# Layer attention scores as three products of high and low parts, in place of fp32 products

## The chip, the cores and the metric

The kernel runs on one core of a Trainium2 chip. The metric is the device time of one execution in microseconds. Three executions of the kernel before gave 2423.75, 2425.5 and 2428.22 us, so the median is 2425.5 us.

## The reference

The program computes a modulated attention block over states of 4 x 1024 tokens and 256 channels, and then a block with two identical layers. Only those layers are touched here. In each layer a token's channels are shifted, projected to 8 heads of 64 channels, normalised and rotated, and every window of 128 tokens attends to itself and to the window before it:

```python
q = l2norm(q) * qs
k = l2norm(k) * ksc
q, k = rotary_xpos(q, k)
...
bq = q.reshape(b, h, w, WINDOW, d) * QK_SCALE
bk, bv = (look_around(bk), look_around(bv))     # the window and the one before it: 256 keys
sim = jnp.einsum('bhwid,bhwjd->bhwij', bq, bk)
...
sim = jnp.where(mask, -jnp.finfo(sim.dtype).max, sim)
attn = jax.nn.softmax(sim, axis=-1)
out = jnp.einsum('bhwij,bhwjd->bhwid', attn, bv)
```

The einsum that makes `sim` is the subject: for each window and head it multiplies 128 queries by 256 keys over 64 channels. After the attention of a layer come an output projection, a normalisation and a gated feed-forward part.

## The kernel before, in words

The function `phase_layers` handles both layers. A layer has 32 tiles of 128 tokens, one window each, and a loop over them in which every engine has its own program. Nothing is scheduled by a tool: the order of each engine's work is the order in which its block calls the small functions, and semaphores tie the engines together (`after(engine, name, n)` waits, `hold` waits and then counts a tick). The loop is pipelined over several tiles. While tile t is attended, the queries and keys of tile t+1 are rotated and transposed, tile t+2 is projected, and the stream of tile t+3 is transposed.

The parts that matter, with TensorE called PE, VectorE DVE, ScalarE ACT and GpSimd POOL:

- `qk_T` (PE, L1754) transposes the rotated queries of the next tile into the PSUM bank `ps_misc` and, a little later, its keys into the bank `ps_qkv[2]`.
- `copy_queries` (ACT, L1346) moves the queries to `qT` in SBUF and signals `qT_done`. `copy_keys` (DVE, L1534) moves the keys to `kT` and signals `kT_done`. `kT` has two halves, so that the window before stays at hand.
- `stream_T` (PE, L1731) writes to `ps_misc` again, so it waits for `qT_done`.
- `scores` (PE, L1762) does the products of two heads for one pair number j from 0 to 3. The first head has rows 0 to 63 of the array and its own PSUM bank, the second has rows 64 to 127 and another bank. Scores 0 and 1 of tile t+1 stand near the end of tile t, behind a wait for `kT_done`; scores 2 and 3 follow early in the next tile. In the text, the first group is scores 0 and 1 and the second group is scores 2 and 3.
- `maxima` (DVE, L1546 and L1549) adds the mask and takes row maxima, `exps` (ACT, L1355) exponentiates, `probs_T` (PE, L1773) transposes, `copy_probs` (ACT, L1363) copies, `values` (PE, L1783) multiplies by the values, and `reciprocals_T` (L1793), `copy_reciprocals` (ACT, L1367) and `normalise_out` (DVE, L1565) divide by the sums.
- `project_out` (PE, L1800) is the output projection, and `add_attended` (DVE, L1569) adds it to the stream. `squared_norms` (DVE, L1503 and L1505) follows on squares from ACT (L1342). The order of DVE in a tile is: rotate queries, normalise keys, maxima 2, `add_attended`, rotate keys, maxima 3, in every second tile a mask copy (L1671), squared norms, `copy_keys`, reciprocal sums, `stream_lo`, squared norms, maxima 0 and 1 of the next tile, `normalise_out`.

An fp32 product is one instruction in the program and two matmul records in the trace. Elsewhere in the kernel products are already made of high and low parts: a value x is rounded to the type fp32r (the high part), the low part is x less that, and `three_products` (L74 to L76) adds high by high, high by low and low by high.

Of the kernel before, what the change touches and what calls it, by code (L numbers as in the profile page):

```python
# [18 lines left out]
ALU = mybir.AluOpType  # L19
# [4 lines left out]
P = 128  # L24
# [1009 lines left out]
def phase_layers(nc, io, scr, keep):  # L1034
# [5 lines left out]
    with ExitStack() as ctx:  # L1040
# [37 lines left out]
        def cut(start, *shape, of=opnd):  # L1078
# [3 lines left out]
            if len(shape) > 1:  # L1082
# [3 lines left out]
        qT, o = cut(o + o % 2, 2, LP, P, of=plain)  # L1086
        kT, o = cut(o, LP, 2 * P, of=plain)
# [37 lines left out]
                 "h_hi ex_done sq_done pt_done rT_done qT_done v_done "  # L1125
# [5 lines left out]
        ACT_SEMS = "h_hi ex_done sq_done pt_done rT_done qT_done v_done w_hi_done warmed ff_done f_hi gl_done"  # L1131
        DVE_SEMS = ("mx_done nb_done h_lo rc_done rB_done oT_done red_done fl_done ra_done kn_done kT_done xa_done msk "
# [40 lines left out]
        with nc.Block() as block:  # L1173
# [42 lines left out]
            def _(pool):  # L1216
# [55 lines left out]
                for l in range(L):  # L1272
# [5 lines left out]
                    pool.memset(kT[:, :, P:2 * P], 0.0).then_inc(s["kz_done"], 1)  # L1278
# [44 lines left out]
            def _(act):  # L1323
# [20 lines left out]
                def copy_queries(l, t, par):  # L1344
                    hold(act, s["tick"], (s["qkT_mm"], at(2 * nth_rotated(l, t) + 1)))
                    act.activation(qT[:, par], ps_misc[:].rearrange("p (j q) -> p j q", j=LP), ACT.Copy).then_inc(s["qT_done"], 1)  # L1346
# [50 lines left out]
                for l in range(L):  # L1397
# [8 lines left out]
                    copy_queries(l, 0, 0)  # L1406
                    squares(l, 1, 1)
# [9 lines left out]
                    with act.Fori(0, B) as b, act.Fori(0, TB // 2) as jj:  # L1417
                        for par in range(2):
                            t = b * TB + jj * 2 + par
                            g = nth(l, t)  # L1420
                            exps(l, t, g, 0, par)
                            exps(l, t, g, 1, par)
                            copy_probs(g, 0)
                            copy_probs(g, 1)
                            copy_values(l, t + 2, (jj * 2 + par + 2) % V_RING)
                            exps(l, t, g, 2, par)
                            squares(l, t + 2, 1)
                            copy_queries(l, t + 1, 1 - par)
                            exps(l, t, g, 3, par)
                            copy_probs(g, 2)  # L1430
                            stream_hi(l, t + 3, 1 - par)
                            squares(l, t + 2, 0)
                            copy_probs(g, 3)
                            copy_reciprocals(g)
# [23 lines left out]
            def _(dve):  # L1458
# [73 lines left out]
                def copy_keys(l, t, par):  # L1532
                    after(dve, "qkT_mm", 2 * nth_rotated(l, t) + 2)
                    dve.tensor_copy(kT[:, :, par * P:(par + 1) * P],  # L1534
                                    ps_qkv[2][:].rearrange("p (j q) -> p j q", j=LP)).then_inc(s["kT_done"], 1)
# [89 lines left out]
                for l in range(L):  # L1625
# [14 lines left out]
                    if l == 0:  # L1640
                        last_shifts()
                    squared_norms(l, 1, 1)
                    copy_keys(l, 0, 0)
# [12 lines left out]
                    with dve.Fori(0, B) as b, dve.Fori(0, TB // 2) as jj:  # L1656
                        for par in range(2):
# [16 lines left out]
                            copy_keys(l, t + 1, 1 - par)  # L1674
# [48 lines left out]
            def _(pe):  # L1723
# [33 lines left out]
                def scores(l, t, j, par):  # L1757
                    if j % 2 == 0:
                        after(pe, "mx_done", 2 * nth_scores(l, t, j))
                    for h in range(2):  # L1760
                        rws = slice(h * DH, (h + 1) * DH)
                        step = pe.matmul(ps_s[h][:, (j % 2) * 2 * P:(j % 2 + 1) * 2 * P], qT[rws, par, j, :], kT[rws, j, :], start=True, stop=True,  # L1762
                                         skip_group_check=True)
                    step.then_inc(s["sc_mm"], 1)
# [263 lines left out]
```

## Time and profile before

| quantity | value |
|---|---|
| median of three executions | 2425.5 us |
| the profiled execution, its own time | 2426.99 us |
| its span, first to last instruction | 2425.2 us |
| mean granted TensorE clock | 0.98 of full |
| PE busy | 2288.2 us (94%) |
| PE weight loads (PEld) busy | 1753.3 us (72%) |
| DVE busy | 1957.4 us (81%) |
| ACT busy | 1551.4 us (64%) |
| POOL busy | 604.0 us (25%) |
| attention loop of the first layer | about 1031 to 1473 us of the span |
| attention loop of the second layer | about 1717 to 2180 us of the span |

The span leaves 1.8 us around it. PE is the busiest engine, but matmul records overlap each other, so a full PE row means only that it seldom waits. The distances between the starts of its records say more than their lengths. The two attention loops together take about 900 us, some 37% of the span; the rest is the first block (to about 990 us), two feed-forward parts and the output.

### The profile page before, as it was taken

The page shows a single profiled execution, that of the slowest core. Times are in us where ns is not written, and L with a number is a line of the kernel's source. Part 1 is how long each engine was busy: PE and PEld are TensorE (multiplying, and loading weights), DVE is VectorE, ACT ScalarE, POOL GpSimd, SP SyncE. Part 2 cuts the span into 40 slices and gives each one's busy share as a digit, 9 for nine tenths or more (in the row PEclk, how much of TensorE's full clock was granted, in tenths as well). Part 3 has the DMA queues.
Part 4 walks back from the last instruction along what each step waited for, and adds up shares of the span by engine and source line. Part 5 has one row for each costly group of instructions (what it writes and reads, how often), then busy time and mean ns, then how long its engine had stood idle before and what let it go on. Part 6 is the DMA issues. An engine that isn't in the chain of part 4 may idle for free. (4 is left out here: it accounts for less than half of the span.)

```text
span 2425.2 us, 63570 instructions
## 1 busy us (share of the span) xinstructions
PE 2288.2 (94%) x21268; PEld 1753.3 (72%) x21268; DVE 1957.4 (81%) x4606; ACT 1551.4 (64%) x3018; POOL 604.0 (25%) x692
## 2 busy tenths in 40 slices
PE   6999999999999999699999997999899999998994
PEld 4767776676777776577777776888677777776884
DVE  6999799979998998688888886666788888885666
ACT  5777577757776775377777674443677777773442
POOL 1000000000000000255555552222545454551110
PEclk9999999999999999899999998999999999998997
DMA  4000100010011001200000000001000000000004
GB/s 130 29 19 13 59 14 19 13 59 21 13 48 49 14 13 45 94 1 2 7 5 4 7 1 28 27 0 40 8 0 9 0 9 0 9 0 10 0 0 139
DMA packets 66986, 58.06 MB, mean 24 GB/s; under 512 B 3812, under 2 KB 64348, under 8 KB 66656
## 3 DMA queue, kind: packets, MB, share of 16 engines
q1 hardware_dynamic: 66912, 57.07, 7.5%
q8 instruction: 47, 0.77, 0.1%
q14 instruction: 27, 0.22, 0.0%
HBM read 44.47 MB, written 8.40 MB: 22 GB/s over the span
## 5 line engine op out<-in xcount | busy, mean ns | idle before, releaser
L599 ACT ACTIVATE at_p<-at_ps_s,at_shift 128x1024 f32<-128x1024 f32 (+3 forms) x384 | 335.7, 899 | 91.2 <-PE at_ps_s L800 49.9
L340 DVE TENSOR_TENSOR at_p_lo<-at_p,at_p_hi 128x1024 f16<-128x1024 f32 (+3 forms) x384 | 357.2, 951 | 5.5
L1355 ACT ACTIVATE ly_probs<-ly_masked,ly_small,ly_rq 128x256 f32<-128x256 f32 x512 | 301.4, 594 | 2.6 <-DVE ly_small L1549 1.4
L828 PE MATMUL at_ps_o<-at_v,at_p_hi 128*128 128x65 f16 x2304 | 238.1, 193 | 3.4 <-DVE at_p_lo L340 2.5
L1249 POOL TENSOR_TENSOR ly_rope_a<-ly_rope_a,ly_rope_t 128x512 f32<-128x512 f32 x132 | 168.8, 1278 | 285.5 <-DVE ly_rope_t L1517 285.5
L828 PEld LDWEIGHTS at_ps_o<-at_v,at_p_hi 128*128 128x128 f16 x2304 | 210.6, 96 | 39.7 <-issue 27.2
L829 PE MATMUL at_ps_o<-at_v,at_p_hi 128*128 128x64 f16 x2304 | 237.2, 194 | 0.0
L830 PE MATMUL at_ps_o<-at_v,at_p_lo 128*128 128x65 f16 x2304 | 236.1, 192 | 0.0
L335 DVE CAST at_p_hi<-at_p 128x1024 f16<-128x1024 f32 (+3 forms) x384 | 206.5, 556 | 25.8 <-ACT at_p L599 14.3
L1363 ACT ACTIVATE ly_operands_plain<-ly_ps 128x512 f32<-128x512 f32 x256 | 152.5, 596 | 102.5 <-PE ly_ps L1773 99.2
L830 PEld LDWEIGHTS at_ps_o<-at_v,at_p_lo 128*128 128x128 f16 x2304 | 212.4, 99 | 0.0
L829 PEld LDWEIGHTS at_ps_o<-at_v,at_p_hi 128*128 128x128 f16 x2304 | 212.1, 97 | 0.0
L1546 DVE CUSTOM_DVE_ANT_0 ly_masked<-ly_ps,ly_mask 128x256 f32<-128x256 f32 x520 | 199.1, 421 | 10.2 <-ACT ly_probs L1355 4.3
L74 PE MATMUL ly_ps<-ly_a_hi,ly_operands 128*128 128x512 f32 x408 | 180.9, 443 | 14.5 <-issue 9.1
L605 ACT ACTIVATE at_stage<-at_ps_m,at_bias 128x512 f32<-128x512 f32 x192 | 131.5, 685 | 77.5 <-PE at_ps_m L76 70.4
L1773 PE MATMUL ly_ps<-ident,ly_probs 128*128 128x128 f32 x1024 | 160.6, 279 | 16.0 <-ACT ly_probs L1355 15.7
L74 PE MATMUL at_ps_m<-at_hT,at_w_hi 128*128 128x512 f32 (+1 forms) x384 | 169.2, 441 | 5.9 <-DVE at_hT L390 3.0
L75 PE MATMUL ly_ps<-ly_a_lo,ly_operands 128*128 128x512 f32 x408 | 164.3, 403 | 0.0
L1773 PEld LDWEIGHTS ly_ps<-ident,ly_probs 128*128 128x128 f32 x1024 | 117.6, 140 | 64.5 <-issue 49.4
L76 PE MATMUL ly_ps<-ly_a_hi,ly_operands 128*128 128x512 f32 x408 | 163.0, 400 | 0.0
L1783 PE MATMUL ly_ps<-ly_operands_plain,ly_values 128*64 128x128 f32 x2048 | 154.2, 282 | 0.0
L75 PE MATMUL at_ps_m<-at_hT,at_w_hi 128*128 128x512 f32 (+1 forms) x384 | 152.7, 398 | 0.0
(238 smaller groups left out, 6242.2 us busy)
## 6 DMA issues: line engine op xcount, KB each, us to landing
at_w_raw<-in_Wv SPq DMA_DIRECT2D x32, 128.0 KB, 2.1
at_w_raw<-in_Wq SPq DMA_DIRECT2D x32, 128.0 KB, 2.3
at_w_raw<-in_Wk SPq DMA_DIRECT2D x32, 128.0 KB, 2.3
at_xio<-in_states SPq DMA_DIRECT2D x4, 1024.0 KB, 6.4
out_x<-x SPq DMA_DIRECT2D x4, 1024.0 KB, 9.5
out<-stream SPq DMA_DIRECT2D x4, 1024.0 KB, 7.9
ly_shifted<-stream SPq DMA_DIRECT2D x8, 508.0 KB
x<-at_xio SPq DMA_DIRECT2D x3, 1024.0 KB, 4.4
```

The lines of the kernel that those rows point to most:

```text
L74: pe.matmul(out, w_hi, x_hi, start=first, stop=False, skip_group_check=True)
L75: pe.matmul(out, w_hi, x_lo, start=False, stop=False, skip_group_check=True)
L335: dve.tensor_copy(p_hi[u % P_RING][:, :, off:], probs[u % P_RING][:, :, off:]).then_inc(p_hi_done, 1)
L340: dve.tensor_tensor(p_lo[u % P_RING][:, :, off:], probs[u % P_RING][:, :, off:], p_hi[u % P_RING][:, :, off:], ALU.subtract).then_inc(p_lo ...
L599: act.activation(probs[u % P_RING][:, :, off:], ps_s[u % 2][:, :, off:], ACT.Exp, bias=shift[:], scale=SCORE_SCALE).then_inc(exp_done, 1)
L828: pe.matmul(out, ph, ones_hi, start=(kt == 0 and t == 0), stop=False, skip_group_check=True)
L829: pe.matmul(out[:, 0:DH], ph, lo, start=False, stop=False, skip_group_check=True)
L830: step = pe.matmul(out, pl, ones_hi, start=False, stop=(kt == qc * CT + t), skip_group_check=True)
L1249: pool.tensor_tensor(ra[:, i, :], ra[:, i, :], rt[:, i, :], ALU.add).then_inc(s["add_done"], 1)
L1355: step = act.activation(pr[:, j % 2, h, :], sm[:, j % 2, h, :], ACT.Exp, bias=small[:, j % 2, 1, h:h + 1], scale=rq[:, par, 2 * j + h:2 * ...
L1546: dve.tensor_tensor_reduce(sm[:, j % 2, h, :], ps_s[h][:, half], mask[:, par].rearrange("p a b -> p (a b)"), 1.0, -3.0e38, ALU.add, ALU.ma ...
L1773: step = pe.transpose(ps_pt[:, (2 * slot + h) * P:(2 * slot + h + 1) * P], pr[:, j % 2, h, slot * P:(slot + 1) * P], ident[:])
```

## The change

The score products stop being fp32. Queries and keys are each kept as a high and a low part of type fp32r, and the score is the sum of high by high, high by low and low by high, accumulated in PSUM. The high parts are made by ACT (for the queries the same copy as before, now rounding; for the keys a new copy), the low parts by DVE, which subtracts the high part from the PSUM bank. `qT_done` and `kT_done` are now signalled by DVE. At the start of each layer the cleared half of `kT` is twice as large.

```diff
-        qT, o = cut(o + o % 2, 2, LP, P, of=plain)
-        kT, o = cut(o, LP, 2 * P, of=plain)
+        qT, o = cut(o + o % 2, 2, 2, LP, P)
+        kT, o = cut(o, 2, LP, 2 * P)
...
-                    pool.memset(kT[:, :, P:2 * P], 0.0).then_inc(s["kz_done"], 1)
+                    pool.memset(f32(kT[:, :, :, P:2 * P]), 0.0).then_inc(s["kz_done"], 1)
...
                 def copy_queries(l, t, par):
                     hold(act, s["tick"], (s["qkT_mm"], at(2 * nth_rotated(l, t) + 1)))
-                    act.activation(qT[:, par], ps_misc[:].rearrange("p (j q) -> p j q", j=LP), ACT.Copy).then_inc(s["qT_done"], 1)
+                    act.activation(qT[:, par, 0], ps_misc[:].rearrange("p (j q) -> p j q", j=LP), ACT.Copy).then_inc(s["qT_hi"], 1)
+
+                def copy_keys(l, t, par):
+                    after(act, "qkT_mm", 2 * nth_rotated(l, t) + 2)
+                    act.activation(kT[:, 0, :, par * P:(par + 1) * P],
+                                   ps_qkv[2][:].rearrange("p (j q) -> p j q", j=LP), ACT.Copy).then_inc(s["kT_hi"], 1)
...
                     copy_queries(l, 0, 0)
+                    copy_keys(l, 0, 0)
                     squares(l, 1, 1)
...
                             exps(l, t, g, 3, par)
                             copy_probs(g, 2)
+                            copy_keys(l, t + 1, 1 - par)
                             stream_hi(l, t + 3, 1 - par)
...
-                def copy_keys(l, t, par):
-                    after(dve, "qkT_mm", 2 * nth_rotated(l, t) + 2)
-                    dve.tensor_copy(kT[:, :, par * P:(par + 1) * P],
-                                    ps_qkv[2][:].rearrange("p (j q) -> p j q", j=LP)).then_inc(s["kT_done"], 1)
+                def low_queries(l, t, par):
+                    after(dve, "qT_hi", nth_rotated(l, t) + 1)
+                    dve.tensor_tensor(qT[:, par, 1], ps_misc[:].rearrange("p (j q) -> p j q", j=LP), f32(qT[:, par, 0]),
+                                      ALU.subtract).then_inc(s["qT_done"], 1)
+
+                def low_keys(l, t, par):
+                    after(dve, "kT_hi", nth_rotated(l, t) + 1)
+                    cols = slice(par * P, (par + 1) * P)
+                    dve.tensor_tensor(kT[:, 1, :, cols], ps_qkv[2][:].rearrange("p (j q) -> p j q", j=LP), f32(kT[:, 0, :, cols]),
+                                      ALU.subtract).then_inc(s["kT_done"], 1)
...
                     rotate_k(l, 0, 0)
                     if l == 0:
                         last_shifts()
+                    low_queries(l, 0, 0)
                     squared_norms(l, 1, 1)
-                    copy_keys(l, 0, 0)
+                    low_keys(l, 0, 0)
...
                             squared_norms(l, t + 2, 1)
-                            copy_keys(l, t + 1, 1 - par)
+                            low_queries(l, t + 1, 1 - par)
+                            low_keys(l, t + 1, 1 - par)
                             reciprocal_sums(g, par)
...
-                    for h in range(2):
-                        rws = slice(h * DH, (h + 1) * DH)
-                        step = pe.matmul(ps_s[h][:, (j % 2) * 2 * P:(j % 2 + 1) * 2 * P], qT[rws, par, j, :], kT[rws, j, :], start=True, stop=True,
-                                         skip_group_check=True)
+                    for n, (qx, kx) in enumerate(((0, 0), (0, 1), (1, 0))):
+                        for h in range(2):
+                            rws = slice(h * DH, (h + 1) * DH)
+                            step = pe.matmul(ps_s[h][:, (j % 2) * 2 * P:(j % 2 + 1) * 2 * P], qT[rws, par, qx, j, :], kT[rws, kx, j, :],
+                                             start=(n == 0), stop=(n == 2), skip_group_check=True)
                     step.then_inc(s["sc_mm"], 1)
```

How the instructions stand on the engines shows it at three places. The first is PE at the end of a tile: the transposes of the stream (`ly_xs`), values 1, the transposes of the probabilities 3, and then the first group of the next tile's scores. Before:

```order
L1731 MATMUL ly_ps<-ident,ly_xs 128x128 x2
L1783 MATMUL ly_ps<-ly_operands_plain,ly_values 64x128 x4
L1142 REGISTER_ALU
L1773 MATMUL ly_ps<-ident,ly_probs 128x128 x4
L1142 ISA
L1762 MATMUL ly_ps<-ly_operands_plain 128x256 x4
L1783 MATMUL ly_ps<-ly_operands_plain,ly_values 64x128 x8
```

The same place on PE now, where `ly_operands` is the area of type fp32r:

```order
L1746 MATMUL ly_ps<-ident,ly_xs 128x128 x2
L1799 MATMUL ly_ps<-ly_operands_plain,ly_values 64x128 x4
L1142 REGISTER_ALU
L1789 MATMUL ly_ps<-ident,ly_probs 128x128 x4
L1142 ISA
L1778 MATMUL ly_ps<-ly_operands 128x256 x12
L1799 MATMUL ly_ps<-ly_operands_plain,ly_values 64x128 x8
```

Nothing else moved on PE; the group has 12 instructions in place of 4, which were fp32. The second place is DVE between the squared norms and the reciprocal sums. Before:

```order
L1503 TENSOR_REDUCE ly_norm<-ly_sq 128x8
L1505 TENSOR_SCALAR ly_norm<-ly_norm 128x8
L1142 REGISTER_ALU
L1534 COPY ly_operands_plain<-ly_ps 128x4x128
L1142 REGISTER_ALU
L1555 RECIPROCAL ly_rsum<-ly_sums 128x8
L1557 COPY ly_operands_plain<-ly_rsum 128x512
```

On DVE now:

```order
L1510 TENSOR_REDUCE ly_norm<-ly_sq 128x8
L1512 TENSOR_SCALAR ly_norm<-ly_norm 128x8
L1541 TENSOR_TENSOR ly_operands<-ly_ps,ly_operands 128x512
L1547 TENSOR_TENSOR ly_operands<-ly_ps,ly_operands 128x4x128
L1142 REGISTER_ALU
L1568 RECIPROCAL ly_rsum<-ly_sums 128x8
L1570 COPY ly_operands_plain<-ly_rsum 128x512
```

One copy became two subtractions, first the queries' and then the keys'. The third place is ACT after the last exponentials of a tile, from the copy of probabilities 2 to the squares. Before:

```order
L1363 ACTIVATE ly_operands_plain<-ly_ps 128x512
L50 REGISTER_ALU
L50 ISA
L50 REGISTER_ALU
L1336 ACTIVATE ly_operands<-ly_ps 128x128
L1337 ACTIVATE ly_operands<-ly_ps 128x128
```

On ACT now:

```order
L1368 ACTIVATE ly_operands_plain<-ly_ps 128x512
L1142 REGISTER_ALU
L1350 ACTIVATE ly_operands<-ly_ps 128x4x128
L50 REGISTER_ALU
L50 ISA
L50 REGISTER_ALU
L1336 ACTIVATE ly_operands<-ly_ps 128x128
L1337 ACTIVATE ly_operands<-ly_ps 128x128
```

ACT has one more copy per tile (L1350, the high part of the keys), between the copy of probabilities 2 and `stream_hi`.

## Rows read from the trace of the kernel before

**Rows 1.** One line's instructions, the mask copy of every second tile: count, length, first and last start.

```profile
L1671 DVE COPY ly_mask<-ly_prev_mask x16: 216/216/216, 1047.9 to 1471.4; 128x128 f32 x16
...
L1671 DVE COPY ly_mask<-ly_prev_mask x16: 214/216/216, 1736.3 to 2176.3; 128x128 f32 x16
```

**Rows 2.** Timeline of PE over one tile: start, length, engine, operation, count.

```profile
1291.15 1.13 PE L1762 MATMUL ly_ps<-ly_operands_plain 64*128 64x256 f32 x8
...
1303.33 0.60 PE L1754 MATMUL ly_ps<-ident,ly_rope_a 128*128 128x128 f32 x4
1303.77 0.38 PE L1731 MATMUL ly_ps<-ident,ly_xs 128*128 128x128 f32 x2
...
1305.26 1.13 PE L1762 MATMUL ly_ps<-ly_operands_plain 64*128 64x256 f32 x8
1306.32 1.09 PE L1783 MATMUL ly_ps<-ly_operands_plain,ly_values 128*64 128x128 f32 x16
```

**Rows 3.** Timelines of PE and its weight loads (PEld): other kinds of product.

```profile
1296.77 1.89 PE L1800 MATMUL ly_ps<-ly_operands_plain 128*128 128x256 f32 x8
...
1503.95 0.28 PE L75 MATMUL ly_ps<-ly_f_lo,ly_operands 128*128 128x256 f32 x1
1504.07 0.28 PE L76 MATMUL ly_ps<-ly_f_hi,ly_operands 128*128 128x256 f32 x1
...
600.68 0.34 PE L800 MATMUL at_ps_s<-at_q1hi,at_k1hi 64*128 64x384 f16 x2
600.85 0.33 PE L800 MATMUL at_ps_s<-at_q1lo,at_k1hi 64*128 64x384 f16 x2
...
1305.79 0.19 PEld L1762 LDWEIGHTS ly_ps<-ly_operands_plain 64*128 64x128 f32 x2
```

**Rows 4.** Timeline of DVE over the same tile; in brackets idle time before and releaser.

```profile
1289.87 0.69 DVE L1534 COPY ly_operands_plain<-ly_ps 128x512 f32<-128x512 f32 x1 [1.04 <-PE ly_ps L1754]
...
1297.99 0.16 DVE L1549 SCALAR_TENSOR_TENSOR ly_small<-ly_small,ly_rq 128x2 f32<-128x2 f32 x1
1298.88 0.42 DVE L1569 TENSOR_TENSOR stream<-stream,ly_ps 128x256 f32 x1 [0.73 <-PE ly_ps L1800]
...
1302.42 0.69 DVE L1503 TENSOR_REDUCE ly_norm<-ly_sq 128x8 f32<-128x512 f32 x1 [0.23 <-DVE ly_mask L1671]
1303.15 0.17 DVE L1505 TENSOR_SCALAR ly_norm<-ly_norm 128x8 f32<-128x8 f32 x1
1303.97 0.69 DVE L1534 COPY ly_operands_plain<-ly_ps 128x512 f32<-128x512 f32 x1 [0.65 <-PE ly_ps L1754]
```

**Rows 5.** Timeline of ACT: two copies in a row, and probabilities 2.

```profile
1285.08 0.60 ACT L1363 ACTIVATE ly_operands_plain<-ly_ps 128x512 f32<-128x512 f32 x1 [1.57 <-PE ly_ps L1773]
1285.57 0.59 ACT L1350 ACTIVATE ly_values<-ly_ps 128x512 f32 x1
...
1303.60 0.60 ACT L1363 ACTIVATE ly_operands_plain<-ly_ps 128x512 f32<-128x512 f32 x1
```

**Rows 6.** Timelines of ACT, DVE and PE at two handovers between engines.

```profile
1308.14 0.60 ACT L1367 ACTIVATE ly_operands_plain<-ly_ps 128x512 f32<-128x512 f32 x1 [2.12 <-PE ly_ps L1793]
...
1308.78 0.69 DVE L1565 TENSOR_TENSOR ly_operands_plain<-ly_ps,ly_operands_plain 128x512 f32<-128x512 f32 x1 [0.23 <-ACT ly_operands_plain L1367]
...
1691.73 0.28 DVE L1496 TENSOR_TENSOR ly_operands<-ly_ps,ly_operands 128x128 fp32r<-128x128 f32 x1
...
1692.11 0.74 PE L74 MATMUL ly_ps<-ly_a_hi,ly_operands 128*128 128x512 f32 x1 [1.33 <-issue]
```

**Rows 7.** Second layer: ACT's timeline, and PE's waits from 1740 to 2180 us.

```profile
1772.33 1.28 ACT L1355 ACT_TABLE_LOAD   x1
...
PE ly_ps L1773 <- ACT ly_probs L1355: 15.7, 15, 1.2
```

**Rows 8.** Timelines of ACT and DVE ahead of the first layer's loop.

```profile
1016.73 0.60 ACT L1342 ACTIVATE ly_sq<-ly_ps 128x512 f32<-128x512 f32 x1 [1.86 <-PE ly_ps L76]
...
1018.16 0.68 DVE L1534 COPY ly_operands_plain<-ly_ps 128x512 f32<-128x512 f32 x1
```

More of the change, by code:

```diff
@@ L1124, in phase_layers @@
                  "xT_mm qkv_mm sc_mm pt_mm pv_mm qkT_mm rT_mm wo_mm "
-                 "h_hi ex_done sq_done pt_done rT_done qT_done v_done "
+                 "h_hi ex_done sq_done pt_done rT_done qT_hi kT_hi qT_done v_done "
                  "mx_done nb_done h_lo rc_done rB_done oT_done red_done fl_done ra_done kn_done kT_done xa_done msk "
@@ L1130, in phase_layers @@
         PE_SEMS = "xT_mm qkv_mm sc_mm pt_mm pv_mm qkT_mm rT_mm wo_mm fT_mm gu_mm y_mm"
-        ACT_SEMS = "h_hi ex_done sq_done pt_done rT_done qT_done v_done w_hi_done warmed ff_done f_hi gl_done"
-        DVE_SEMS = ("mx_done nb_done h_lo rc_done rB_done oT_done red_done fl_done ra_done kn_done kT_done xa_done msk "
+        ACT_SEMS = "h_hi ex_done sq_done pt_done rT_done qT_hi kT_hi v_done w_hi_done warmed ff_done f_hi gl_done"
+        DVE_SEMS = ("mx_done nb_done h_lo rc_done rB_done oT_done red_done fl_done ra_done kn_done qT_done kT_done xa_done msk "
                     "w_lo_done rope_q bn ag vr nr xnd f_lo uf_done u_lo ya_done")
```

## The prediction

> **What bounds the kernel now.** I read the mask copy's starts first, because it runs once in two tiles and so gives the period of the loop [rows 1]. In the first layer 15 pairs of tiles take 1471.4 - 1047.9 = 423.5 us, or 14.12 us a tile. In the second layer they take 440.0 us, or 29.33 us a pair: 1.1 us more for each pair. Then I read PE through a tile. From one first group of scores to the next, 1291.15 to 1305.26, is 14.11 us [rows 2], and in the first layer's loop PE's timeline shows no idle time that another engine causes. DVE, by contrast, waits for PE: 0.73 us ahead of `add_attended`, 0.65 or 1.04 us ahead of the copy of keys [rows 4]. So PE is the bound of the first layer. In the second layer ACT loads an activation table of 1.28 us once in a pair, and PE waits 15.7 us in 15 waits for the exponentials behind it, 1.05 us a pair [rows 7]. There ACT is the bound for a short stretch, between the first and the second group of scores' followers. The change makes PE's score groups shorter, lengthens the way from transposed keys to scores, and gives DVE one more operation. I count these in turn, on a clock that starts at 0 with a first group of scores.
>
> **Score groups on PE.** A group before takes 1.06 us to the start of what follows (1305.26 to 1306.32), in 8 records of 1.13 us together [rows 2]. The output projection has records of the same width over all 128 rows: 8 of them take 1.89 us [rows 3]. The seven steps between starts are thus (1.89 - 1.13) / 7 = 0.109 us shorter in the scores. That fits when the two heads run beside each other: an unpaired step of 0.217 us, and a pair of records in 0.217 us. A group is then 4 pair steps, 0.87 us, and 0.19 us of start and handover that I leave as they are.
>
> Now a group has 12 instructions, 6 pairs of one pass each. No row shows fp32r products on 64 rows. The nearest is the first block's f16 scores, also two heads on 64 rows: a pair with 384 columns is followed by the next after 0.17 us [rows 3], which for 256 columns makes 0.113 us. fp32r with 256 columns on all rows steps by 0.12 us [rows 3]. Paired, 6 steps are 0.68 us (with 0.12 us: 0.72; with half of 0.217: 0.65), so a group saves 0.19 us, with ends of 0.15 and 0.22. Unpaired, 12 steps of 0.12 are 1.44 us, and a group costs 0.57 us more. I take 0.19, as the row with two heads and one pass is the nearest in kind. Two groups a tile save 0.38 us.
>
> **The way of the keys.** Before, DVE took up the transposed keys at 1303.97 and the scores began at 1305.26, 1.29 us later, without waiting: the transposes of the stream, values 1 and probabilities 3 filled that time. Now ACT copies first. It starts its copy of probabilities 2 at 1303.60, and its next copy can start 0.49 us later [rows 5], at 1304.09, 0.12 us after the keys are there. The copy takes 0.60 us, the handover to DVE 0.04 us (1308.14 + 0.60 to 1308.78), a DVE operation on a PSUM bank and SBUF 0.69 us, and the handover from DVE to PE 0.10 us (1691.73 + 0.28 to 1692.11) [rows 6]. The sum is 0.12 + 0.60 + 0.04 + 0.69 + 0.10 = 1.55 us. The slack that hid the old copy is used up, and the scores wait 0.26 us. Behind them in PE's queue stand values 2 and 3 and all of the next tile. The ends are 0.12 us (if ACT is free at once and handovers cost nothing) and 0.40 us. Without a mask copy, a first-layer tile thus changes by -0.38 + 0.26 = -0.12 us.
>
> **The way of the queries, and DVE.** `stream_T` now waits for a subtraction on DVE. DVE starts on the keys 0.79 us ahead of the scores, at -0.79. From there to where it is free for `add_attended` was 1298.15 - 1289.87 = 8.28 us [rows 4], the subtraction being as long as the old copy: 7.49. PE had the projection ready at 1298.88 - 1291.15 = 7.73, and now has it at 7.35, so DVE's wait of 0.73 us is gone and DVE itself is 0.14 us late. From `add_attended` to the end of the squared norms (1298.88 to 1303.32) are 4.44 us in a tile with the mask copy: 11.93. With 0.69 and 0.10 the low queries reach PE at 12.72, where PE wants to start the transposes of the stream at 1303.77 - 1291.15 - 0.38 = 12.24. PE waits 0.48 us there, and 1.49 us later, at 14.21, the scores begin. The keys alone would have allowed 12.82 - 0.38 + 1.55 = 13.99. So the tile with the mask copy takes 14.21 us, 0.10 us more than before. In the other tile the mask copy and the wait behind it (0.44 us together) are missing, and the queries come in time. The pair changes by -0.02 us, the 16 pairs of the first layer by -0.3 us.
>
> **The second layer.** In the tile with the table load PE waits for ACT after its second group of scores, and the table load hangs on ACT's last copy of the tile before, which only the first group brings forward. The second group's saving falls into PE's wait of 1.05 us. The tile changes by -0.19 + 0.26 = +0.07 us, the one with the mask copy again by +0.10, and 16 pairs by +2.7 us.
>
> **Ahead of each loop.** ACT's copy of the keys now stands ahead of squares that DVE waits for, and DVE's keys wait for it too. Before, the squares began as soon as PE had finished a projection, at 1016.73, and the keys' copy at 1018.16 ran right before the first scores [rows 8]. One ACT copy of 0.60 us and a handover in the chain make 0.75 us a layer by my estimate, 1.5 us in all, between 0 and twice 1.39 us (a copy, a subtraction and a handover in line). The larger clearing on POOL is covered: the keys come much later. The extra ACT copy inside the loop is covered by ACT's waits for PE, of which [rows 5] shows one of 1.57 us; the copy of probabilities 3 has to wait for PE's transposes anyway.
>
> **Sum.** -0.3 + 2.7 + 1.5 = +3.9 us. The profiled execution took 2427.0 us by its own time (span 2425.2), which makes 2430.9; against the median of 2425.5 it makes 2429.4 us.
>
> **Rivals.**
>
> 1. The handovers stay hidden and the whole saving lands. For it: DVE and ACT both have idle time. Against it: the slack that counts is 1.29 us, and three operations in line don't fit. First layer 32 x 0.38 = 12.2 us, second 16 x (0.19 + 0.38) = 9.1 us, less 1.5: 2405.7 us.
> 2. The heads don't pair in fp32r: slower. Price 0.57 us a group. For it: no row has this kind on 64 rows. Against it: both fp32 and f16 pair [rows 2, 3]. First layer 32 x (1.14 + 0.26) = 44.8 us; second, where one group's loss hides in the wait for ACT, 16 x (0.83 + 1.40) = 35.7 us; with 1.5: 2507.5 us. It decides as soon as a pair takes more than about 0.15 us.
> 3. The weight loads limit the pairs. A pair of loads is recorded with 0.19 us [rows 3]; until now a pair of products of 0.217 us covered it, and 0.113 us would not. If pairs step by 0.19, a group is 1.14 us, 0.27 more: 32 x 0.80 + 16 x 1.33 + 1.5 = 48.4, or 2474 us. Against it: part of a record is lead-in, since the fp32 pairs show no gap. The Trainium skill, "TensorE: Matmul & The Clock Gate", Part 3, says that a weight load overlaps a matmul in flight only when its row group differs. Here each head's next load has its own head's product in flight; by that rule a pair would cost load and product in line, 0.19 + 0.217 = 0.41 us before, and four pairs 1.63 us, where the whole group took 1.06. The trace does not agree for fp32.
> 4. DVE becomes the bound of every tile. It has lost its wait ahead of `add_attended`, and in the tile with the mask copy it sets the pace already. If its stretches of 8.28 and 4.44 us grow by 0.1 us each, for instance as operations meet POOL's, it costs 0.2 us in each of 64 tiles, 12.8 us more than the forecast: 2442 us.
>
> **Chances and range.** The forecast, with errors of a few us around it, 56 in 100; DVE as the bound 19; unpaired heads 10; the full saving 6; loads as the limit 4; something that I don't see 5. 0.1 us a tile are 6.4 us, and 0.2% of the time, what a measurement of this kernel can tell from no change, are 4.9 us. The forecast lies inside that and close to its upper edge. The range is 2418 to 2446 us: below lies the full saving, above unpaired heads and loads. From the same cases: faster 0.09, no change 0.41, slower 0.50.
>
> **What would show it.** In the profile after, a first group of scores should be some 0.87 us long to the next start, with pairs about 0.11 to 0.12 us apart. DVE's wait ahead of `add_attended` should be gone in the first layer, PE should show new waits ahead of the stream's transposes in every second tile and ahead of the scores in the others, and the mask copies should stand 28.2 us apart in the first layer and 29.5 us in the second. The forecast is wrong if groups take over 1.06 us, if PE has no new wait, or if the queries' subtraction is late in both kinds of tile.

## The result and the profile after

The changed kernel takes 2433.3 us (median of 9 executions, 2429.0 to 2433.5), the kernel before 2424.0 us (median of 9, 2422.3 to 2428.2) on the same chip. The ratio is 1.0032, with a 95% interval of 1.0022 to 1.0043: 7.8 us slower by the ratio, with 5.3 to 10.4 (the two medians lie 9.3 us apart). The forecast was 3.9 us slower, below that interval, and its range of 2418 to 2446 us holds the measured time. Every ratio in this text is to the kernel before on the same chip. The profiled execution took 2431.27 us by its own time (span 2429.2, mean granted clock 0.98 as before).

The first rows are the busy times on the page of the changed kernel, and then the mask copy of every second tile, which answers to [rows 1].

```profile
PE 2273.0 (94%) x21788; PEld 1762.2 (73%) x21788; DVE 1988.6 (82%) x4672; ACT 1573.8 (65%) x3084; POOL 602.1 (25%) x692
```

```profile
L1685 DVE COPY ly_mask<-ly_prev_mask x16: 214/215/271, 1045.2 to 1470.5; 128x128 f32 x16
L1685 DVE COPY ly_mask<-ly_prev_mask x16: 214/215/216, 1736.6 to 2179.4; 128x128 f32 x16
```

PE has 15 us less of busy time and the kernel is slower, so PE waits somewhere it did not. The mask copies divide the difference by place. The first number is taken from DVE's first weight subtraction of the layers, which starts at 996.0 us before and at 993.0 after:

| stretch | before, us | after, us | difference |
|---|---|---|---|
| weight subtraction to first mask copy | 51.9 | 52.2 | +0.3 |
| 15 pairs of tiles, first layer | 423.5 | 425.3 | +1.8 |
| from loop to loop | 264.9 | 266.1 | +1.2 |
| 15 pairs of tiles, second layer | 440.0 | 442.8 | +2.8 |
| last mask copy to the end | 248.9 | 249.8 | +0.9 |
| sum | 1429.2 | 1436.2 | +7.0 |

The first block, which the change doesn't touch, ran 3 us shorter in this one profile, and so the two own times are only 4.3 us apart. In a second profile of the same changed kernel the subtraction starts at 995.6 us. The sum of the table is the number to hold against the medians.

PE over a pair of tiles, which answers to [rows 2]: start, length, engine, line, operation, count, idle time before with its releaser.

```profile
1289.95 0.98 PE L1778 MATMUL ly_ps<-ly_operands 64*128 64x256 f32 x12 [0.20 <-DVE ly_operands L1547]
1290.85 1.09 PE L1799 MATMUL ly_ps<-ly_operands_plain,ly_values 128*64 128x128 f32 x16
...
1301.82 0.60 PE L1769 MATMUL ly_ps<-ident,ly_rope_a 128*128 128x128 f32 x4
1302.70 0.41 PE L1746 MATMUL ly_ps<-ident,ly_xs 128*128 128x128 f32 x2 [0.28 <-DVE ly_operands L1541]
...
1304.21 0.98 PE L1778 MATMUL ly_ps<-ly_operands 64*128 64x256 f32 x12
1305.12 1.09 PE L1799 MATMUL ly_ps<-ly_operands_plain,ly_values 128*64 128x128 f32 x16
...
1318.31 0.39 PE L1778 MATMUL ly_ps<-ly_operands 64*128 64x256 f32 x2 [0.20 <-DVE ly_operands L1547]
```

A score group now lasts 0.90 to 0.91 us to the start of the next work (1289.95 to 1290.85, 1304.21 to 1305.12) where it lasted 1.06. The two new waits stand in the brackets: for the queries' low part (L1541) in the tile with the mask copy, for the keys' low part (L1547) in the other. The tile with the mask copy takes 1304.21 - 1289.95 = 14.26 us, the other 1318.31 - 1304.21 = 14.10 us.

DVE and ACT in the same pair, which answer to [rows 4] and [rows 5].

```profile
1289.11 0.69 DVE L1547 TENSOR_TENSOR ly_operands<-ly_ps,ly_operands 128x512 fp32r<-128x512 f32 x1 [1.19 <-ACT ly_operands L1350]
1297.37 0.42 DVE L1582 TENSOR_TENSOR stream<-stream,ly_ps 128x256 f32 x1 [0.28 <-PE ly_ps L1816]
1300.97 0.69 DVE L1510 TENSOR_REDUCE ly_norm<-ly_sq 128x8 f32<-128x512 f32 x1 [0.23 <-DVE ly_mask L1685]
1301.78 0.68 DVE L1541 TENSOR_TENSOR ly_operands<-ly_ps,ly_operands 128x512 fp32r<-128x512 f32 x1
1303.20 0.69 DVE L1547 TENSOR_TENSOR ly_operands<-ly_ps,ly_operands 128x512 fp32r<-128x512 f32 x1 [0.75 <-ACT ly_operands L1350]
```

```profile
1302.09 0.60 ACT L1368 ACTIVATE ly_operands_plain<-ly_ps 128x512 f32<-128x512 f32 x1
1302.58 0.59 ACT L1350 ACTIVATE ly_operands<-ly_ps 128x512 fp32r<-128x512 f32 x1
```

ACT's copy of the keys (1302.58) starts right behind its copy of probabilities 2. DVE waits for it 0.75 us and subtracts at 1303.20.

The waits of the first layer's loop (1060 to 1480 us): who waited, for whom, us in all, times, longest. The last row is PE's wait for the exponentials in the second layer (1740 to 2180 us), which answers to [rows 7].

```profile
PE ly_ps L1746 <- DVE ly_operands L1541: 3.4, 15, 0.3
PE ly_ps L1778 <- DVE ly_operands L1547: 3.1, 15, 0.2
...
DVE ly_operands L1547 <- ACT ly_operands L1350: 29.8, 30, 1.2
DVE stream L1582 <- PE ly_ps L1816: 10.8, 29, 0.5
...
PE ly_ps L1789 <- ACT ly_probs L1360: 18.1, 15, 1.4
```

The idle time in brackets is shorter than what a wait costs, since a record's length reaches past the point where the next could start. From starts: the two transposes of the keys' rotation (L1769) are followed after 0.88 us where the wait is (1301.82 to 1302.70) and after 0.43 us where there is none. The queries' wait thus costs 0.44 us a pair. The wait for keys costs 0.27 us a pair in the same way.

### The profile page after: what moved, and what is told of

Its sections match the earlier page's. It is cut to its first block and busy times, and to the rows that moved or that the text cites. A ratio compares the mean times of both kernels' runs of the same rounds, so it can differ in the third digit from the quotient of the medians.

```text
span 2429.2 us, 64792 instructions
## 1 busy us (share of the span) xinstructions
PE 2273.0 (94%) x21788; PEld 1762.2 (73%) x21788; DVE 1988.6 (82%) x4672; ACT 1573.8 (65%) x3084; POOL 602.1 (25%) x692
## 5 line engine op out<-in xcount | busy, mean ns | idle before, releaser
L1789 PE MATMUL ly_ps<-ident,ly_probs 128*128 128x128 f32 x1024 | 160.7, 279 | 18.5 <-ACT ly_probs L1360 18.1
L1799 PE MATMUL ly_ps<-ly_operands_plain,ly_values 128*64 128x128 f32 x2048 | 154.2, 282 | 0.0
```

The source lines that it names most:

```text
L1789: step = pe.transpose(ps_pt[:, (2 * slot + h) * P:(2 * slot + h + 1) * P], pr[:, j % 2, h, slot * P:(slot + 1) * P], ident[:])
```

## The experiments

The theory: the products save 0.15 us a group of scores, 0.60 us a pair of tiles, and the two new ways to PE cost 0.27 + 0.44 us, so a pair loses a little. The rivals: the products save nothing much and something else costs; or DVE's added operation is the bound. I give for each kernel the pair distance in the first and second layer, from the mask copies as above. It is 28.23 and 29.33 us before, 28.35 and 29.52 after.

**The products alone.** Queries and keys are moved as in the kernel before, as high parts only, and all three products are of high parts. The low parts are left out, and with them two DVE subtractions and ACT's copy of keys. The diff is against the changed kernel: the removed `copy_keys` are ACT's, the added ones are DVE's copy of the kernel before.

```diff
-                    copy_keys(l, 0, 0)
...
-                            copy_keys(l, t + 1, 1 - par)
...
-                    low_queries(l, 0, 0)
                     squared_norms(l, 1, 1)
-                    low_keys(l, 0, 0)
+                    copy_keys(l, 0, 0)
...
-                            low_queries(l, t + 1, 1 - par)
-                            low_keys(l, t + 1, 1 - par)
+                            copy_keys(l, t + 1, 1 - par)
...
-                    for n, (qx, kx) in enumerate(((0, 0), (0, 1), (1, 0))):
+                    for n, (qx, kx) in enumerate(((0, 0), (0, 0), (0, 0))):
```

> Scores as three fp32r products, but all three of high by high, so that no low part is made or read (the low parts are left out of the computation). Queries and keys are copied as before the change: ACT copies the queries, DVE the keys. Theory (the products are cheaper and the new handovers take that back): each group of scores is 0.15 us shorter, as in the profile after; first layer 32 x 0.30 = 9.6 us, second 16 x 0.45 = 7.2 us, so about 2407 us against 2424 before, and mask copies 27.6 us apart in the first layer. Rival (the products bring nothing, since something else than PE sets the tile): about 2424 us, mask copies 28.2 us apart.

Measured: 2405.7 us (4 executions, 2405.0 to 2408.9), ratio 0.9928 (0.9913 to 0.9944). The pairs take 27.63 and 28.87 us. PE over a tile:

```profile
1289.18 0.98 PE L1763 MATMUL ly_ps<-ly_operands 64*128 64x256 f32 x12
...
1299.07 0.98 PE L1763 MATMUL ly_ps<-ly_operands 64*128 64x256 f32 x12
1299.98 1.09 PE L1784 MATMUL ly_ps<-ly_operands_plain,ly_values 128*64 128x128 f32 x16
```

The group is 0.91 us long, as in the changed kernel, and no score waits. The products are worth 0.72% of the time, 17 us; in the profiles the 15 pairs of each layer are 9.1 and 6.9 us shorter. The rest of the change then costs the 1.0032 - 0.9928 that remain, 25 us.

**The two parts and their handovers alone.** ACT and DVE work as in the changed kernel, and the score is one fp32 product of the high parts. It leaves the low parts out of the scores.

```diff
-                    for n, (qx, kx) in enumerate(((0, 0), (0, 1), (1, 0))):
-                        for h in range(2):
-                            ... qT[rws, par, qx, j, :], kT[rws, kx, j, :], start=(n == 0), stop=(n == 2)
+                    for h in range(2):
+                        ... f32(qT[rws, par, 0, j, :]), f32(kT[rws, 0, j, :]), start=True, stop=True
```

> The high and low parts are made and handed over as in the changed kernel, but the scores are one fp32 product of the high parts (the low parts are made and left out of the product). Theory: the keys reach PE 0.30 us late in each tile, and the queries about 0.44 us late in tiles with the mask copy, and nothing is saved: 16 x 0.74 in each layer and 1.5 us ahead of the loops, about 25 us more than before, 2449 us. Rival (the handovers wait only because the products became short): 2424 to 2430 us.

Measured: 2448.6 us (2446.3 to 2449.9), ratio 1.0101 (1.0085 to 1.0116), pairs of 28.95 and 30.00 us. The waits of PE in the first loop:

```profile
PE ly_ps L1746 <- DVE ly_operands L1541: 3.1, 14, 0.3
PE ly_ps L1777 <- DVE ly_operands L1547: 3.1, 15, 0.2
```

The handovers cost 1.01% of the time, 24.5 us. With the products alone this closes the square for a pair of the first layer: 28.23 before, -0.60 for the products, +0.72 for the handovers, and both together 28.35. In the second layer 29.33 - 0.46 + 0.67 makes 29.54, and both together take 29.52. The same waits are there with the old products, so it isn't the new products that make PE wait.

**The queries' low part earlier.** On DVE, the subtraction goes right behind maxima 3, ahead of the mask copy and the squared norms.

```diff
                             maxima(l, t, g, 3, par)
+                            low_queries(l, t + 1, 1 - par)
...
-                            low_queries(l, t + 1, 1 - par)
                             low_keys(l, t + 1, 1 - par)
```

> The changed kernel with DVE's subtraction for the queries moved ahead of the mask copy and the squared norms. Theory: the wait ahead of the stream's transposes (0.28 us in each tile with the mask copy) goes, and that tile falls from 14.26 to the 14.10 us that the keys allow: 32 x 0.16 = 5 us less than the changed kernel, about 2428 us. Rival (DVE's own work is the bound of a tile): no change, 2433 us.

Measured: 2428.2 us (2425.4 to 2431.1), ratio 1.0019 (1.0010 to 1.0028), pairs of 28.23 and 29.39 us. The waits of PE in the first loop:

```profile
PE ly_ps L1778 <- DVE ly_operands L1547: 6.8, 30, 0.2
```

The wait for queries is gone from all tiles, and the wait for keys, 15 times before, now occurs 30 times. PE comes to the keys 0.44 us earlier in the tile with the mask copy, and the keys don't.

**Work moved into the wait for keys.** To the early queries comes one move on PE: values 2 ahead of the wait for keys, behind probabilities 3.

```diff
                             values(g, 1, v_slots)
                             probs_T(g, 3)
+                            values(g, 2, v_slots)
                             after(pe, "kT_done", nth_rotated(l, t + 1) + 1)
                             scores(l, t + 1, 0, 1 - par)
                             scores(l, t + 1, 1, 1 - par)
-                            values(g, 2, v_slots)
                             values(g, 3, v_slots)
```

> As queries_early, and on PE values 2 stands ahead of the wait for the keys and of the first group of scores. Theory: the 0.5 us of values 2 covers the keys' way, no wait is left, and the whole saving of the products lands: 2424 - 16.8 + 1.5, about 2409 us, with mask copies 27.6 us apart in the first layer. Rival (DVE's own work is the bound, which has one operation of 0.6 us more): the tile stays near 14.1 us, 2428 us.

Measured: 2419.0 us (2418.0 to 2421.2), ratio 0.9981 (0.9972 to 0.9990), pairs of 27.93 and 29.15 us. No wait for keys or queries is left, and yet 10 us are missing from the forecast. PE in one tile:

```profile
1299.86 0.66 PE L1799 MATMUL ly_ps<-ly_operands_plain,ly_values 128*64 128x128 f32 x8
1300.45 0.97 PE L1778 MATMUL ly_ps<-ly_operands 64*128 64x256 f32 x12
1301.35 0.66 PE L1799 MATMUL ly_ps<-ly_operands_plain,ly_values 128*64 128x128 f32 x8
1301.94 0.66 PE L1809 MATMUL ly_ps<-ident,ly_operands_plain 128*128 128x128 f32 x4
```

Values 2 and 3 cost 0.59 us each to the next start. In one run of 16 records they cost 1.03 us together (1305.12 to 1306.15 in the changed kernel). Cutting the run costs 0.15 us a tile, 0.30 a pair, which is the difference from 27.63.

**The same, without the cut.** Values 2 goes next to values 1, ahead of probabilities 3, so that two runs of values become one of 16 and one of 8, as before.

```diff
                             values(g, 1, v_slots)
+                            values(g, 2, v_slots)
                             probs_T(g, 3)
```

> As values_first, but values 2 stands right behind values 1, and the transposes of probabilities 3 come after both. Theory: values_first lost 0.15 us in each tile because it cut the run of values 2 and 3 in two (0.59 + 0.59 us in place of 1.03); here values 1 and 2 form one run, so 64 x 0.15 = 9.6 us come back: about 2409.5 us, mask copies 27.6 us apart in the first layer. Rival (DVE's own work sets the pace at 27.9 us a pair): no better than 2419 us.

Measured: 2413.9 us (5 executions, 2410.3 to 2416.5), ratio 0.9954 (0.9940 to 0.9968), pairs of 27.63 and 28.86 us: those of the products alone.

```profile
1296.93 0.38 PE L1746 MATMUL ly_ps<-ident,ly_xs 128*128 128x128 f32 x2
1297.24 1.09 PE L1799 MATMUL ly_ps<-ly_operands_plain,ly_values 128*64 128x128 f32 x16
1298.27 0.66 PE L1789 MATMUL ly_ps<-ident,ly_probs 128*128 128x128 f32 x4
1298.85 0.97 PE L1778 MATMUL ly_ps<-ly_operands 64*128 64x256 f32 x12
```

No row has a bracket. DVE has all of its added work here and the pairs are as short as without it, so DVE's added operation isn't the bound. This is faster than the kernel before (the interval lies below 1) and does all that the changed kernel does. Between the loops and behind the second it is still some 6 us longer than the products alone (266.0 against 263.6 us, 249.6 against 246.0 us). The output transfers, in the products alone and here:

```profile
2388.71 9.07 SPq L992 DMA_DIRECT2D out<-stream  x4
...
2396.41 5.67 SPq L992 DMA_DIRECT2D out<-stream  x4
```

They start 230.5 us behind the last mask copy there and 235.5 us here. From the end of DVE's last addition (L1007) to the end of the span are 6.8 us there and 9.7 us here, and 9.7 us in the kernel before. So 2.9 of the 6 us lie in the output, which the change doesn't touch; why the transfers start earlier in that one profile is not shown. For the other 3 us no run here names the operation.

**Keys ahead of probabilities 2 on ACT**, with the early queries.

```diff
-                            copy_probs(g, 2)
                             copy_keys(l, t + 1, 1 - par)
+                            copy_probs(g, 2)
```

> As queries_early, and on ACT the high part of the keys is copied ahead of the copy of probabilities 2. Theory: ACT then starts on the keys as soon as they are there, which takes 0.1 us out of their way, and PE's wait for them (0.2 us in each tile) shortens by as much: about 6 us less than queries_early, 2422 us. Rival (the wait hangs on DVE's order, not on the way through ACT): 2428 us.

Measured: 2440.5 us (2438.5 to 2442.0), ratio 1.0062 (1.0049 to 1.0076), a clear miss. ACT and PE:

```profile
1307.29 0.60 ACT L1350 ACTIVATE ly_operands<-ly_ps 128x512 fp32r<-128x512 f32 x1 [0.40 <-PE ly_ps L1769]
1307.78 0.59 ACT L1368 ACTIVATE ly_operands_plain<-ly_ps 128x512 f32<-128x512 f32 x1
```

```profile
1308.52 0.63 PE L1789 MATMUL ly_ps<-ident,ly_probs 128*128 128x128 f32 x4 [0.46 <-ACT ly_operands_plain L1368]
1309.08 0.98 PE L1778 MATMUL ly_ps<-ly_operands 64*128 64x256 f32 x12
```

The scores no longer wait for the keys. But ACT idles 0.40 us until the keys are transposed, and then its copy of probabilities 2 is late, which frees the PSUM bank that PE's transposes of probabilities 3 write. The expectation counted only what the keys gain and not what else waits for the copy of probabilities 2.

**The heads one after the other in the program.** The loop over heads goes outside the loop over products.

```diff
-                    for n, (qx, kx) in enumerate(((0, 0), (0, 1), (1, 0))):
-                        for h in range(2):
+                    for h in range(2):
+                        for n, (qx, kx) in enumerate(((0, 0), (0, 1), (1, 0))):
```

> The changed kernel with the three products of the first head issued before the three of the second, instead of head by head in alternation. Theory (the alternation lets two heads run beside each other): a group then takes 12 single steps of 0.12 us, 0.72 us more than now; 32 x 1.44 in the first layer and 16 x (0.72 + 1.44) in the second, about 80 us more, 2513 us. Rival (a step is set by issue or by loads, whatever the order): 2433 us.

Measured: 2433.3 us (2431.6 to 2434.0), ratio 1.0033 (1.0021 to 1.0045). The first theory, that the order in the program pairs the heads, is refuted: the group is as long as in the changed kernel.

```profile
1292.96 0.98 PE L1778 MATMUL ly_ps<-ly_operands 64*128 64x256 f32 x12 [0.21 <-DVE ly_operands L1547]
```

**Both heads on the same rows.** So I put the second head's products on the first head's 64 rows. The scores of the second head are left out.

```diff
-                            rws = slice(h * DH, (h + 1) * DH)
+                            rws = slice(0, DH)
```

> Both heads' products are taken from the same 64 rows (head 0's queries and keys), in the order of the changed kernel; the scores of head 1 are left out, so the output is another. Everything else is as in the changed kernel. If the two heads run beside each other because they lie on different rows, whatever their order in the program (theory A, after the heads in turn cost nothing), nothing can run beside anything here: the group of 12 products takes 12 x 0.113 = 1.36 us instead of 0.91, +0.90 us a tile, of which the waits for keys and queries (0.2 and 0.28) can swallow up to 0.4: over 60 tiles +30 to +54, so 2463 to 2487. If a product of 64 rows simply takes 0.075 us and nothing runs beside anything (theory B), the group stays at 0.91 and the time at 2433.

Measured: 2511.3 us (2508.1 to 2513.0), ratio 1.0357 (1.0340 to 1.0374), pairs of 31.14 and 31.66 us.

```profile
1289.14 1.69 PE L1778 MATMUL ly_ps<-ly_operands 64*128 64x256 f32 x12
1290.76 0.66 PE L1789 MATMUL ly_ps<-ident,ly_probs 128*128 128x128 f32 x4
```

The group takes 1.62 us against 0.91. Its record is 1.69 - 0.98 = 0.71 us longer for six more steps, 0.118 us a step: the 0.12 us of fp32r on all rows [rows 3]. Two heads on different rows do run beside each other, in either order, and it is worth 78 us. In the trace of the heads in turn, too, the records of a group start in pairs, 0.01 us apart. The size was missed: the expected 1.36 us are 12 steps of 0.113 and leave out the 0.19 us of start and handover that the prediction counts (12 x 0.12 + 0.19 = 1.63). The fourfold 0.71 us a pair is 2.84 us, and the pair grew by 31.14 - 28.35 = 2.79: next to nothing of it was swallowed by waits.

**The order of PE alone**, with the low queries late, and **the same order in the kernel before**. The edit is that of the kernel without the cut, on the changed kernel and on the kernel before.

> The changed kernel with one thing moved on TensorE: values 2 right behind values 1, ahead of the transposes of probabilities 3 and of the wait for keys. The low part of the queries stays behind the copy of the mask. The early queries were worth 4.5 us alone and the order 14.3 on top of them: if the two add up, 2433 - 14.3 = 2418.5, with no wait of TensorE for keys left and the 0.28 us before the transposes of the stream still there in every second tile. Rival: the order's free time swallows the queries too: 2414, the time of both together. Rival: without early queries the keys are late all the same: 2428 or more.

> The kernel before with the same move of values 2. It has no wait for keys to remove (TensorE arrives there after the keys), and the runs of values stay as they are, one of 16 and one of 8 records. Expected: 2424, within 3 us of the kernel before. Rival: the order helps by itself, through what DVE and ACT get earlier: 2414, and then the products are worth nothing.

Measured: the changed kernel with the order alone 2423.8 us (10 executions, 2422.3 to 2426.3), ratio 0.9998 (0.9988 to 1.0007), pairs of 28.07 and 29.27 us. The kernel before, so reordered, 2427.1 us (10 executions, 2420.9 to 2429.4), ratio 1.0008 (0.9998 to 1.0017). PE in the changed kernel with the order alone:

```profile
1299.58 0.60 PE L1769 MATMUL ly_ps<-ident,ly_rope_a 128*128 128x128 f32 x4
1300.41 0.41 PE L1746 MATMUL ly_ps<-ident,ly_xs 128*128 128x128 f32 x2 [0.23 <-DVE ly_operands L1541]
1300.75 1.09 PE L1799 MATMUL ly_ps<-ly_operands_plain,ly_values 128*64 128x128 f32 x16
```

The forecast of 2418.5 failed because I added the two gains as if they were independent. Against the changed kernel's 28.35 us, a pair of the first layer gains 0.12 us by the early queries alone, 0.28 by the order alone and 0.72 by both (by the ratios 3, 8 and 19 us of the whole). Early queries alone give 0.3 of their 0.44 us back at the keys, where the wait now comes twice a pair. Once something fills the time ahead of the keys, they keep it. And the reordered kernel before has nothing to fill and gains nothing, so the gain over it is that of the products.

**Repeats.** The changed kernel once more, and the kernel without the cut once more.

> The changed kernel once more, beside the others on the same chip: 2431 to 2433 us, and in its trace the layers (from DVE's first subtraction of weights to the end) again 7 us longer than before, with the first block where chance puts it.

> The same kernel as values_paired, once more beside the three others: 2411 to 2416, faster than the kernel before by 8 to 13 us and than before_reordered by as much if the gain is that of the products.

Measured: 2432.7 us (2430.6 to 2433.4), ratio 1.0028 (1.0017 to 1.0040), and 2412.9 us (2411.6 to 2416.1), ratio 0.9955 (0.9938 to 0.9972). The pairs of the changed kernel are 28.34 and 29.53 us in the second profile.

## Why the prediction was right, step by step

**What bounds.** Right: PE in both layers, but for its wait for the exponentials in the second, and what came of the change was decided by PE's waits and not by busy times.

**Score groups.** The direction and the pairing were right, the size was at its lower end: a group saves 0.15 us and not 0.19. The pair step is that of fp32r on all rows, 0.12 us [rows 3], and not the f16 pair's scaled to 256 columns. This is the mis-sized term. The first layer's pair came out at +0.12 instead of -0.02, 15 of them at +1.8 instead of -0.3 us. By the runs of the parts, the four groups save 0.60 us a pair and not 0.76, and the handovers cost 0.72 and not 0.74. A right size of the group alone would not have mended the sum: there it enters only the tile without the mask copy (14.10 us instead of 13.99, 0.08 of it by its two groups and 0.03 by the keys), since the prediction let the other tile hang on DVE alone (14.26 instead of 14.21, see the queries). The row of the same kind of product, with another number of rows, would have been the better neighbour than the row with the same rows and another type.

**The way of the keys.** 0.26 us predicted, 0.27 measured. ACT's copy of the keys does start right behind probabilities 2 (0.49 us later), and DVE follows. The handover from DVE to PE is 1289.95 - (1289.11 + 0.69) = 0.15 us and not 0.10; that from ACT to DVE is 1303.20 - (1302.58 + 0.59) = 0.03 us and not 0.04. The whole way is 0.12 + 0.59 + 0.03 + 0.69 + 0.15 = 1.58 us instead of 1.55.

**The way of the queries.** The tile with the mask copy was predicted at 14.21 us and takes 14.26. The low queries let PE start 1302.70 - 1289.95 = 12.75 us after the scores, predicted 12.72. One part on the way there failed: DVE's wait ahead of `add_attended` is not gone but shrank from 0.73 to 0.28 us, in the first loop from 21.2 to 10.8 us. DVE comes there 7.98 us after its start on the keys (1297.37 - 0.28 - 1289.11), not 8.28. The two stretches of DVE from the first maxima to `normalise_out`, before and after:

```profile
1292.49 0.42 DVE L1546 CUSTOM_DVE_ANT_0 ly_masked<-ly_ps,ly_mask 128x256 f32<-128x256 f32 x1
1294.72 0.69 DVE L1565 TENSOR_TENSOR ly_operands_plain<-ly_ps,ly_operands_plain 128x512 f32<-128x512 f32 x1
...
1291.75 0.42 DVE L1559 CUSTOM_DVE_ANT_0 ly_masked<-ly_ps,ly_mask 128x256 f32<-128x256 f32 x1
1293.65 0.69 DVE L1578 TENSOR_TENSOR ly_operands_plain<-ly_ps,ly_operands_plain 128x512 f32<-128x512 f32 x1
```

That took 2.23 us and takes 1.90, which is the difference. The view shows no wait in it: the wait of 0.23 us for ACT's reciprocals [rows 6] stands in the other tile, so what shortened this stretch stays open. PE's projection thus still releases `add_attended`, 1297.37 - 1289.95 = 7.42 us after the scores, and through it this tile hangs on the groups too (7.73 - 2 x 0.15 = 7.43); the prediction had DVE free at 7.49. The subtraction started 1301.78 - 1289.95 = 11.83 us after the scores (predicted 11.93), and the handover to PE took 0.21 us (from 1301.78 + 0.68 to the weight load at 1302.67) where I had put 0.10. The errors nearly cancel, so that 12.72 came out as 12.75 is in part luck.

**The second layer.** 29.50 us predicted, 29.52 measured. The second group's saving did fall into PE's wait for the exponentials: that wait grew from 15.7 to 18.1 us in 15 times, 0.16 us each, a group's 0.15. The close agreement is in part luck: by the runs of the parts the products save 0.46 us a pair and not 0.57, and the handovers cost 0.67 and not 0.74.

**Ahead of the loops.** 1.5 us predicted, and the two stretches that hold the starts of the loops grew by 0.3 and 1.2 us. The total fits by luck. In the first layer the squared norms do come late, by 1.2 us counted from the first weight subtraction (995.98 to 1017.36 before, 992.95 to 1015.54 after). But DVE then waits for ACT all the same, before and after:

```profile
1023.80 2.29 DVE L1476 TENSOR_TENSOR stream<-stream,modB 128x2048 f32<-128x2048 f32 x1 [0.65 <-ACT stream L1414]
...
1020.79 2.29 DVE L1483 TENSOR_TENSOR stream<-stream,modB 128x2048 f32<-128x2048 f32 x1 [0.25 <-ACT stream L1420]
```

Counted from the same subtraction these start at 27.82 and 27.84 us: nothing of the delay is left ahead of the first loop. At the start of the second layer DVE falls 0.4 us behind, from 0.9 us late at the rotation of the first keys (1702.04 before, 1702.01 after, counted from the last mask copy of the first loop at 1471.4 and 1470.5) to 1.3 us at the first maxima (1710.89 and 1711.26). So the term of 1.5 us measures 0.4. The other 1.1 us are 0.3 in the first tiles of the first loop, 0.4 in its last tile and 0.4 in the feed-forward part, where no run here names the operation. The 0.9 us behind the last mask copy, 0.4 of them in the last tile, I had not counted.

**The sum.** +3.9 us predicted, +7.0 by the table: 2.1 of the difference is the first layer's loop, with the groups' smaller saving as its cause, 0.9 the end, 0.1 the second layer's loop. The sign and what causes it were right; the size was about half of the measured one.

**Rivals.** The full saving (2405.7 us predicted) isn't what happened. With the handovers out of the way the kernel takes 2405.7 too, but the agreement is partly luck: 19.8 us less than before was priced, 17 were measured, and the kernel before stood at 2425.5 us for the one and 2423.2 us for the other. Unpaired heads were priced at 2507.5 and cost 2511.3 when forced. The weight loads don't limit: 12 loads fit in 0.91 us. Here the rule of the Trainium skill, "TensorE: Matmul & The Clock Gate", Part 3, on loads and row groups again does not agree with this trace for fp32r: in the changed kernel each head's next load has that head's product in flight, and a pair still costs 0.12 us. With all products on the same rows the step is 0.118 us as well, so there is no room there for a load in line, which that trace records with 0.18 to 0.19 us. DVE as the bound of every tile did not come: DVE keeps waits of 0.75 and 1.19 us for ACT in each pair.

## What to carry to other kernels

Price the products and the way of their operands apart: here they are worth -17 and +25 us, and one run of each shows it. When an operand gets a second producer in line, look for work that can stand ahead of its wait on the bounding engine, and keep runs of one kind of product whole in doing so; of two waits in line, removing the first moves part of it to the second, so that only both removals together bring the whole gain (0.12 and 0.28 us a pair alone, 0.72 together). Before two copies are swapped on one engine, list every reader of both and the buffer that each of them frees. Compare a predicted sum with the trace term by term: the 1.5 us ahead of the loops matched in total and measured 0.4 in place.

## What the runs showed of the hardware

- Products of fp32r on 64 rows and 256 columns, two heads on different rows: 12 in 0.91 us. On the same rows: 12 in 1.62 us. The step is 0.118 us, for a pair there and for a single product here. The order in the program, heads alternating or three products of one head and then three of the other, makes no difference (0.98 us recorded, both).
- A run of 16 records of the values' fp32 products (L1799, 128 rows, 64 columns of weights, 128 columns) costs 1.03 us to the next start, two runs of 8 cost 0.59 us each: a cut is worth 0.15 us.
- From the end of a DVE operation to the start of the product that waits for it: 0.15 us for the keys (1289.80 to 1289.95), 0.24 us for the queries (1302.46 to 1302.70), by the records. In starts, a wait that is recorded as 0.20 or 0.28 us costs 0.27 or 0.44 us.
